# Second layer's front: the half-filled second steps of keys' and values' products side by side in two 64-row tiles, values' product moved behind the keys'

## The reference

```python
# second layer, "front": cross-attention with the context, 16 heads of 16
q = (xn @ Wq + bq);  k = (ctx @ Wk + bk);  v = (ctx @ Wv + bv)     # ctx: [128, 192] per sequence
attn = softmax(q k^T / sqrt(16));  out = attn v
x = x + relu(out @ W1 + b1) @ W2 + b2
# second layer, "cell": six nodes, each attention with 8 heads of 32
for c in range(6):
    q, k, v = (node @ We[edge] + be[edge]) * ew[c]   # three earlier nodes
    node[c] = act_w[c] * mha(q, k, v, Wq[c], Wk[c], Wv[c], Wo[c]) + q
x = x + layernorm(node[5]) * g + b
```

## Time and profile before

| | |
|---|---|
| median of 3 runs | 4046.48 us (4045.95 to 4048.25) |
| profiled execution | 4048.74 us, span 4046.9 us |
| mean granted TensorE clock | 0.995 |
| TensorE busy | 3974.8 us, 98% of the span |
| ScalarE, VectorE, GpSimd busy | 66%, 59%, 46% |

### The profile page before, as it was taken

One profiled execution on the slowest core, in us unless ns is written; L12 is line 12 of the kernel. 1 busy time (PEld: TensorE's weight loads), 2 busy tenths in 40 slices (PEclk: granted clock), 3 DMA queues, 4 the chain that ended last, 5 costly groups with the idle time before them and its releaser, 6 DMA issues.

```text
span 4046.9 us, 100880 instructions
## 1 busy us (share of the span) xinstructions
PE 3974.8 (98%) x38276; PEld 3397.6 (84%) x38276; DVE 2400.2 (59%) x6216; ACT 2651.8 (66%) x11851; POOL 1865.0 (46%) x1979
## 2 busy tenths in 40 slices
PE   8999999999999999999999999999999999999998
PEld 6888876678888888888888888888888888888887
DVE  6888861025566666656666666566666656656654
ACT  8998961125666666666666666666666666666765
POOL 5788872113444444444444444444444444444434
PEclk9999999999999999999999999999999999999999
DMA  3232214520000000000000000000000000000000
GB/s 103 75 105 76 72 52 154 168 78 18 12 14 15 15 14 14 13 17 15 14 13 13 14 13 13 19 13 12 13 12 12 12 12 12 12 12 12 7 4 9
DMA packets 117867, 129.74 MB, mean 32 GB/s; under 512 B 12006, under 2 KB 110676, under 8 KB 117264
## 3 DMA queue, kind: packets, MB, share of 16 engines
q1 hardware_dynamic: 105648, 109.80, 8.5%
q0 software_dynamic: 6144, 8.43, 0.7%
q10 hardware_dynamic: 5600, 5.07, 0.4%
HBM read 89.68 MB, written 41.94 MB: 33 GB/s over the span
## 4 chain that ended last, share of the span: by engine, by line
PE 76%; DVE 1%; ACT 0%; POOL 0%; issue 0%; DMA 0%; POOLq 0%
PE c_product L1552 37%; PE c_product L1563 15%; PE c_product L1611 10%; PE c_scores L1601 7%; PE c_product L1634 5%; PE c_product L1622 2%; DVE c_qT L1407 1%; PE c_product L1540 1%; ACT c_front_probs L1364 0%; PE c_product L1671 0%; DMA out<-c_fin 0%; POOL c_fin L1348 0%; DVE c_nodes L1407 0%; POOL c_front_probs L1318 0%; ACT c_probsT L1370 0%
## 5 line engine op out<-in xcount | busy, mean ns | idle before, releaser
L1318 POOL TENSOR_TENSOR c_probs<-c_probs,c_row_inv 128x512 f32<-128x512 f32 x744 | 770.3, 1045 | 1357.0 <-DVE c_row_inv L1419 1351.4
L1364 ACT ACTIVATE c_probs<-c_scores,c_neg_max 128x128 f32<-128x128 f32 x2976 | 1052.6, 407 | 333.1 <-DVE c_neg_max L1416 332.9
L1552 PE MATMUL c_product<-c_nodes,cell_w 128*128 128x256 f32 x4352 | 1065.2, 383 | 2.8 <-DVE c_nodes L1478 2.4
L1552 PEld LDWEIGHTS c_product<-c_nodes,cell_w 128*128 128x128 f32 x4352 | 796.2, 190 | 121.4 <-DVE c_nodes L1407 8.3
L1416 DVE TENSOR_REDUCE c_neg_max<-c_scores 128x4 f32<-128x512 f32 x1024 | 658.9, 680 | 177.6 <-PE c_scores L1601 170.1
L1364 ACT ACTIVATION_READ_ACCUMULATOR c_probs<-c_scores,c_neg_max 128x1 f32 x2976 | 733.1, 246 | 0.0
L1370 ACT COPY c_probsT<-c_product 128x512 f32<-128x512 f32 x744 | 408.1, 602 | 433.9 <-PE c_product L1611 430.4
L1364 ACT ACTIVATE c_front_probs<-c_scores,c_neg_max 128x128 f32<-128x128 f32 x1120 | 399.6, 398 | 182.5 <-DVE c_neg_max L1416 182.5
L1563 PE MATMUL c_product<-cell_w,c_nodes 128*128 128x256 f32 x1792 | 429.3, 379 | 0.0
L1318 POOL TENSOR_TENSOR c_front_probs<-c_front_probs,c_row_inv 128x512 f32<-128x512 f32 x280 | 295.0, 1057 | 291.0 <-DVE c_row_inv L1419 289.3
L474 ACT ACTIVATE a_probs<-a_scores,a_neg_max 128x128 f32<-128x128 f32 x1024 | 360.4, 409 | 47.4 <-DVE a_neg_max L545 47.0
(11 more groups left out here) (181 smaller groups left out, 6449.7 us busy)
## 6 DMA issues: line engine op xcount, KB each, us to landing
e_w<-in_L_ffn_w SPq DMA_DIRECT2D x12, 1024.0 KB, 6.2
a_x<-in_x SPq DMA_DIRECT2D x32, 256.0 KB, 3.0
a_ctxT<-in_ctx_pairsT SPq DMA_DIRECT2D x32, 256.0 KB, 3.5
x<-a_x SPq DMA_DIRECT2D x32, 256.0 KB, 2.1
xn<-a_xn SPq DMA_DIRECT2D x32, 256.0 KB, 2.2
c_routed<-xn SPq DMA_DIRECT2D x32, 256.0 KB, 2.7
c_x<-x SPq DMA_DIRECT2D x32, 256.0 KB, 3.1
c_ctxT<-in_ctx_pairsT SPq DMA_DIRECT2D x32, 256.0 KB, 2.8
```

The lines of the kernel that those rows point to most:

```text
L1318: nc.gpsimd.tensor_tensor(e, e, rinv[:, i, r].unsqueeze(2).broadcast_to([P, 4, T]), ALU.mult).then_inc(norm_made, 1)
L1364: a = nc.scalar.activation(probs(n, j)[:, r, k], S[r][:, k], ACT.Exp, bias=nmax[:, i, r, k:k + 1], accum_out=rsum[:, i, r, k:k + 1])
L1552: i = T_.matmul(m[:, u], w[:, k, u * P:(u + 1) * P], src[:, k], start=n == 0, stop=n == last)
```

## The change

Three things are changed.

1. **The second steps in pairs.** Where `f.V` of a job stands right behind `f.K`, TensorE first does the two 128-row matmuls of keys' first step (`u` = 0, 1), then the two of values' first step, and then, for u = 0 and 1, one keys' matmul on rows 0 to 63 of the second step and one values' matmul on rows 64 to 127. The two of a pair write different banks. Both products' semaphore counts are raised by their last matmul.
2. **The order.** `f.V` moves from behind `K5` to behind `f.K` on TensorE, and `f.V^` from behind `S4.x3` (in the last turns `K5^`) to behind `f.K^` on VectorE. The heads are made longer so that jobs 0 to 2 keep their order, and job 31 keeps its own in the tail. Jobs 3 to 30 take the paired form. ScalarE's and GpSimd's orders stay.
3. **The layout.** The context's rows 128 to 191 stand twice, in rows 128 to 191 and 192 to 255. `Wk` has its last 64 rows in 128 to 191 and zeros behind them; `Wv` has zeros in 128 to 191 and its last 64 rows in 192 to 255. Sizes stay 256 rows. The first layer reads arrays of the same layout with its old code.

```diff
 PE_ORDER = """
...
-S0:0 O2:1 K3:1 T5.0:2 Q3:1 T5.1:2 V0:0 T0.0:0 S3:1 A5:2 f.K:-1 T0.1:0 O5:2 K1:0 T3.0:1 A0:0 f.Sb0:-1 O0:0 V3:1
-T3.1:1 Q1:0 f.Tb0.0:-1 K4:1 A3:1 S1:0 O3:1 V1:0 Q4:1 T1.0:0 S4:1 T1.1:0 K5:1 f.V:-1 f.Tb0.1:-1 V4:1 A1:0
+S0:0 O2:1 K3:1 T5.0:2 Q3:1 T5.1:2 V0:0 T0.0:0 S3:1 A5:2 f.K:-1 f.V:-1 T0.1:0 O5:2 K1:0 T3.0:1 A0:0 f.Sb0:-1
+O0:0 V3:1 T3.1:1 Q1:0 f.Tb0.0:-1 K4:1 A3:1 S1:0 O3:1 V1:0 Q4:1 T1.0:0 S4:1 T1.1:0 K5:1 f.Tb0.1:-1 V4:1 A1:0
...
 DVE_ORDER = """
...
-S0.i1:1 O2^:2 K3^:2 S5.i3:3 S0.i2:1 S0.i3:1 Q3^:2 S3.x0:2 S3.x1:2 A5^:3 S3.x2:2 S3.i0:2 f.K^:0 S3.i1:2 S3.x3:2
-S3.i2:2 O5^:3 K1^:1 S3.i3:2 A0^:1 f.Sb0.x0:0 f.Sb0.x3:0 f.Sb0.x1:0 f.Sb0.x2:0 f.Sb0.i0:0 O0^:1 f.Sb0.i1:0
...
+S0.i1:1 O2^:2 K3^:2 S5.i3:3 S0.i2:1 S0.i3:1 Q3^:2 S3.x0:2 S3.x1:2 A5^:3 S3.x2:2 S3.i0:2 f.K^:0 f.V^:0 S3.i1:2
+S3.x3:2 S3.i2:2 O5^:3 K1^:1 S3.i3:2 A0^:1 f.Sb0.x0:0 f.Sb0.x3:0 f.Sb0.x1:0 f.Sb0.x2:0 f.Sb0.i0:0 O0^:1
...
                 elif n == "f.K":
                     loaded(pe, c_in, early["ctx0_in"], j)
-                    project(product(n, j), (wk, ct)).then_inc(prod, 1)
+                    if after != ("f.V", j):
+                        project(product(n, j), (wk, ct)).then_inc(prod, 1)
+                    else:
+                        keys_m = product(n, j)
+                        for u in range(2):
+                            T_.matmul(keys_m[:, u], wk[:, 0, u * P:(u + 1) * P], ct[:, 0], start=u == 0, stop=False)
                 elif n == "f.V":
                     loaded(pe, c_in, early["ctx0_in"], j)
-                    project_rows(product(n, j), (wv, ct)).then_inc(prod, 1)
+                    m = product(n, j)
+                    if keys_m is None:
+                        project_rows(m, (wv, ct)).then_inc(prod, 1)
+                    else:
+
+                        for b in range(PAIR):
+                            T_.matmul(m[:, b], ct[:, 0, b * T:(b + 1) * T], wv[:, 0], start=b == 0, stop=False)
+                        for u in range(2):
+                            k = T_.matmul(keys_m[:, u], wk[half[0], 1, u * P:(u + 1) * P], ct[half[0], 1], start=False, stop=u == 1)
+                            v = T_.matmul(m[:, u], ct[half[1], 1, u * T:(u + 1) * T], wv[half[1], 1], start=False, stop=u == 1)
+                        k.then_inc(prod, 1)
+                        v.then_inc(prod, 1)
+                        keys_m = None
...
+    arrays["ctx_pairsT"] = np.ascontiguousarray(np.concatenate([c, c[:, P:]], 1))
...
+        gap = np.zeros_like(wk[P:])
+        arrays[n + "_Wk_rows"] = np.concatenate([wk, gap])
+        arrays[n + "_Wv_rows"] = np.concatenate([wv[:P], gap, wv[P:]])
```

More of the change, by code:

```diff
@@ L966 @@
 f.Txn^:1 S5.i1:3 f.Q^:0 S5.x3:3 Q0^:1 K0^:1 A2^:2 S5.i0:3 S0.x0:1 S0.x3:1 S0.x1:1 S5.i2:3 S0.x2:1 S0.i0:1
-S0.i1:1 O2^:2 K3^:2 S5.i3:3 S0.i2:1 S0.i3:1 Q3^:2 S3.x0:2 S3.x1:2 A5^:3 S3.x2:2 S3.i0:2 f.K^:0 S3.i1:2 S3.x3:2
-S3.i2:2 O5^:3 K1^:1 S3.i3:2 A0^:1 f.Sb0.x0:0 f.Sb0.x3:0 f.Sb0.x1:0 f.Sb0.x2:0 f.Sb0.i0:0 O0^:1 f.Sb0.i1:0
-f.x2:-1 Q1^:1 f.Sb0.i2:0 e.st:3 K4^:2 A3^:2 S1.x2:1 S1.x0:1 S1.i2:1 S1.x1:1 S1.x3:1 O3^:2 S1.i0:1 S1.i1:1
-S1.i3:1 Q4^:2 S4.x0:2 f.Sb0.i3:0 S4.x1:2 S4.x2:2 S4.i0:2 K5^:2 S4.x3:2 f.V^:0 A1^:1 S4.i1:2 f.Sb1.x2:0
+S0.i1:1 O2^:2 K3^:2 S5.i3:3 S0.i2:1 S0.i3:1 Q3^:2 S3.x0:2 S3.x1:2 A5^:3 S3.x2:2 S3.i0:2 f.K^:0 f.V^:0 S3.i1:2
+S3.x3:2 S3.i2:2 O5^:3 K1^:1 S3.i3:2 A0^:1 f.Sb0.x0:0 f.Sb0.x3:0 f.Sb0.x1:0 f.Sb0.x2:0 f.Sb0.i0:0 O0^:1
+f.Sb0.i1:0 f.x2:-1 Q1^:1 f.Sb0.i2:0 e.st:3 K4^:2 A3^:2 S1.x2:1 S1.x0:1 S1.i2:1 S1.x1:1 S1.x3:1 O3^:2 S1.i0:1
+S1.i1:1 S1.i3:1 Q4^:2 S4.x0:2 f.Sb0.i3:0 S4.x1:2 S4.x2:2 S4.i0:2 K5^:2 S4.x3:2 A1^:1 S4.i1:2 f.Sb1.x2:0
 f.Sb1.x3:0 S4.i2:2 f.Sb1.x0:0 f.Sb1.i2:0 f.Sb1.x1:0 f.Ab0^:0 S4.i3:2 f.Sb1.i0:0 O1^:1 f.Sb1.i1:0 K2^:1 e.nm:3
@@ L999 @@
 f.Tb1.1:1 Q2:0 f.Ab1:1 S2:0 f.W1a:1 f.W1b:1 f.Tx:2 f.W2:1 V2:0 B16:0 T2.0:0 f.K:2 f.Txn:1 K0:1 Q0:1 T2.1:0
-S0:1 A2:0 O2:0 B17:0 Q3:0 T0.0:1 S3:0 V3:0 f.Q:2 V0:1 T0.1:1 K1:1 f.Sb0:2 A0:1 T3.0:0 O0:1 T3.1:0
+S0:1 A2:0 O2:0 B17:0 Q3:0 T0.0:1 S3:0 V3:0 f.Q:2 V0:1 T0.1:1 K1:1 f.Sb0:2 A0:1 T3.0:0 O0:1 T3.1:0 Q1:1
+f.Tb0.0:2 K4:0 A3:0 S1:1 O3:0 V1:1 Q4:0 T1.0:1 S4:0 T1.1:1 K5:0 f.V:2
 """
@@ L1068 @@
 f.Q^:2 S5.x3:5 Q0^:3 K0^:3 A2^:4 S0.x0:3 S5.i1:5 S0.x2:3 S5.i0:5 S0.x1:3 S5.i2:5 S0.i2:3 S0.i0:3 O2^:4 S5.i3:5
[L1069 to L1075, removed]
+K3^:4 S0.x3:3 Q3^:4 S0.i1:3 f.x2:1 f.st:1 S3.x0:4 S0.i3:3 S3.x1:4 A5^:5 S3.x3:4 f.K^:2 f.V^:2 S3.i1:4 S3.i0:4
+O5^:5 S3.x2:4 K1^:3 A0^:3 S3.i3:4 f.Sb0.x0:2 S3.i2:4 f.Sb0.x3:2 f.Sb0.x1:2 f.Sb0.x2:2 f.Sb0.i0:2 O0^:3
+f.Sb0.i1:2 Q1^:3 f.Sb0.i2:2 A3^:4 S1.x1:3 S1.x0:3 S1.x2:3 S1.x3:3 S1.i1:3 K4^:4 O3^:4 S1.i0:3 S1.i2:3 e.st:5
+S1.i3:3 Q4^:4 S4.x0:4 S4.x2:4 f.Sb0.i3:2 S4.x3:4 S4.x1:4 S4.i0:4 K5^:4 S4.i2:4 A1^:3 f.Sb1.x0:2 S4.i1:4
+S4.i3:4 f.Sb1.x3:2 f.Ab0^:2 f.Sb1.x1:2 f.Sb1.x2:2 f.Sb1.i3:2 f.Sb1.i0:2 f.Sb1.i1:2 O1^:3 f.Sb1.i2:2 K2^:3
+e.nm:5 Q2^:3 A4^:4 S2.x1:3 S2.x0:3 S2.x2:3 S2.x3:3 O4^:4 f.Ab1^:2 f.x:1 Q5^:4 S2.i0:3 S2.i1:3 f.W1a^:2 f.Tx^:1
+f.W1b^:2 S5.x0:4 S2.i2:3 S5.x3:4 S5.x1:4 f.K^:1 S5.i3:4 f.W2^:2 S5.x2:4 S5.i1:4 S2.i3:3 S5.i0:4 f.Q^:1 f.st3:2
 f.Sb0.x3:1 S5.i2:4 f.Sb0.x1:1 f.Sb0.x0:1 f.nm3:2 f.V^:1 f.Sb0.i3:1 f.Txn^:2 f.Sb0.i0:1 f.Sb0.x2:1 f.Sb0.i1:1
@@ L1576, in node_landed @@
                 landed("f.Txn" if c < 0 else f"O{c}", j)
-            for n, j in on_pe:
+            keys_m = None
+            half = slice(0, P // 2), slice(P // 2, P)
+            for (n, j), after in zip(on_pe, on_pe[1:] + [None]):
                 s = j % JOBS_IN_FLIGHT
@@ L1741 @@
           "L1_ffn_Wo", "L1_ffn_ln_g", "L1_ffn_ln_b"]
-def whole_tiles(a, axis):
-    pad = [(0, -a.shape[i] % P if i == axis else 0) for i in range(a.ndim)]
-    return np.ascontiguousarray(np.pad(a, pad))
 def lay_out(inputs):
@@ L1752, in lay_out @@
     c = arrays.pop("ctx_768")
[L1753 to L1756, removed]
+    c = c.reshape(-1, PAIR, *c.shape[1:]).transpose(0, 3, 1, 2).reshape(c.shape[0] // PAIR, c.shape[2], PAIR * c.shape[1])
+    arrays["ctx_pairsT"] = np.ascontiguousarray(np.concatenate([c, c[:, P:]], 1))
+    for n in ("L0_xattn", "L1_xattn"):
+        wk, wv = arrays.pop(n + "_Wk"), arrays.pop(n + "_Wv")
+        gap = np.zeros_like(wk[P:])
+        arrays[n + "_Wk_rows"] = np.concatenate([wk, gap])
+        arrays[n + "_Wv_rows"] = np.concatenate([wv[:P], gap, wv[P:]])
     arrays["mask_BxS2_bf1"] = np.ascontiguousarray(inputs["mask_BxS2_bf1"]).view(np.uint8)
```

## The result

The changed kernel takes 4101.07 us (median of four runs, 4099.79 to 4101.29) against 4046.22 us (4044.94 to 4048.25) for the kernel before in the same measurement: a ratio of 1.0134, 95% interval 1.0117 to 1.0152. The profiled execution took 4101.22 us, its span is 4099.4 us, and the mean granted clock is 0.994 (0.995 before). The forecast was 4097 us. One run stands apart from all others: the fourth run of experiment 7 took 6789.92 us at a mean granted clock of 0.554, and that experiment's ratio and times leave it out.

The account below looks back on a forecast made before the run. TensorE's chain of steps was taken to bound the kernel. Per job, -0.51 + 1.22 + 1.08 = +1.79 us, times 28 is +50.1 us, from 4046.5 to 4096.6 us; range 4060 to 4111, the forecast's own 4085 to 4108.

Parts of the forecast that it names:

- The saving of the pairs: On TensorE at `f.K` and `f.V`, pairing 64-row matmuls saves 0.51 us per job net of tiling changes.
- full overlap: The two 64-row tiles of a pair run side by side on TensorE, saving four records' time, 0.86 us per job.
- the changes of tiling: Entering 64-row tiling once more and returning from it costs TensorE 0.34 us per job.
- The wait at `O5`: TensorE's `O5` waits 1.12 us for VectorE's `f.K^` to free its bank; 1.22 us per job with the weight load.
- the hand-over: Time from the end of `f.K^` on VectorE until the waiting `O5` goes on, taken as 0.05 us.
- The unhidden weight load: After its wait, `O5`'s first weight load is not hidden on TensorE: 0.10 us per job.
- The wait at `f.Sb1`: With `f.V` gone from ahead of it, `f.Sb1` on TensorE waits for ScalarE's exponentials of `S4`: 1.08 us per job.
- The next context's load: SyncE's load leaves about 34 us earlier, has the whole job to land, and changes nothing.
- Only one of the waits: Rival: only the wait at `O5` (+0.71 us per job, 4066 us) or at `f.Sb1` (+0.57, 4063 us) comes; chance 0.12.
- Neither wait lasts: Rival: banks are freed before TensorE asks, so the saving stays: 14 us faster, 4032 us; chance 0.05.
- The tiles don't overlap: Rival: the pairs on TensorE run one after another, 2.22 us more per job, 4109 us; chance 0.07.

Follow-up runs that it names:

- experiment 7: The changed kernel with, in 26 of 28 jobs, both `O5` ahead of `T0.1` and `K2` at `f.V`'s old place: 4068.79 us, ratio 1.0051 (three runs).
- experiment 2: The changed kernel with the pairs' order kept but every matmul of them over all 128 rows, so no tiling: 4108.84 us, ratio 1.0155.
- experiment 3: The changed kernel with both matmuls of a pair on rows 0 to 63, so they can't run side by side: 4112.57 us, ratio 1.0158.
- experiment 4: The changed kernel with `O5` ahead of `T0.1` in 26 of 28 jobs, and three steps of `S3` moved on other engines: 4068.70 us, ratio 1.0056.
- experiment 5: The changed kernel with `O5` ahead of `T0.1` as in experiment 4, but both products in full unpaired form: 4077.45 us, ratio 1.0076.
- experiment 8: The changed kernel with VectorE doing `f.V^` ahead of `f.K^`: 4128.89 us, ratio 1.0203.
- experiment 1: The changed kernel with its new order and layout, but both products in full 128-row form, not interleaved: 4079.00 us, ratio 1.0080.
- experiment 6: The changed kernel with `K2` put at `f.V`'s old place, ahead of `f.Tb0.1`, in 26 of 28 jobs: 4102.65 us, ratio 1.0133.
- experiment 9: The kernel before the change with only the new layout of the context, `Wk` and `Wv`: 4046.72 us, ratio 1.0001.

## Why the prediction was right, step by step

| per job, us | predicted | measured | from |
|---|---|---|---|
| `f.K` to `T0.1` | 3.56 to 2.99: -0.57 | 2989.45 - 2986.46 = 2.99: -0.57 | after |
| `T0.1` to `O5` (0.87 before) | 2.05: +1.18 | 2991.60 - 2989.45 = 2.15: +1.28 | after |
| `O5` to `K1` (3.46 before) | +0.10 | 2995.13 - 2991.60 = 3.53: +0.07 | after |
| `f.Sb1` to `f.Ab0` (1.10 before) | +1.08 | 2.25: +1.15 | after |
| sum | +1.79 | +1.93 (99.50 - 97.58 = 1.92) | |

- **The saving of the pairs.** Right in each part: full overlap (0.85 of 0.86 us) and the changes of tiling (0.28 us up to `T0.1`'s start), by experiments 2 and 3. The prediction took these prices from the rounds of scores and the column tiles, and they held for the 64-row tiles. The net 0.51 becomes 0.47 where a projection follows the pairs and not transposes (0.10 in place of 0.06), and experiments 4 and 5 measure 0.45.
- **The wait at `O5`.** Right in place, releaser and size. The term that was too small is the hand-over. `f.K^` ends at 2990.92 + 0.53 = 2991.45 and `O5` starts at 2991.60, so 0.15 us lie between and not 0.05. In experiment 8, behind a longer wait, it is 0.15 us again (3007.63 + 0.54 = 3008.17 to 3008.32). The 0.05 was read from `S4` at 2982.83, a round of scores, and `O5` is a projection; `f.Sb1`, a round of scores too, goes on after 0.05 us also behind a real wait (3029.35 to 3029.40). Which of the two a step takes was not known from the rows of before. The chain's row of 0.14 us at 2991.46 is this time. The unhidden weight load was a little too large a term: `O5` itself is 0.07 longer and not 0.10.
- **The wait at `f.Sb1`.** Right, by experiment 1 for its size alone (1.15 us with nothing else changed) and by experiment 6, where the filler takes it away. It was 0.07 too small for another reason than at `O5`. The prediction let ScalarE's chain end with the last exponential, at 2991.33. The matmuls wait for the accumulator read behind it, which before the change ends at 2991.43 (the row of 2991.11 shown above). With this end the same working gives 1.18 us, and 1.15 was measured. The hand-over of 0.05 us was right here.
- **The rest.** The next context's load leaves at 2989.59, 3.1 us behind `f.K`'s start; the prediction had it leave some 34 us earlier and cost nothing. `K1` doesn't wait for `f.V^`, and `f.Ab0` doesn't wait behind `f.Tb0`'s copies. Layout and loads cost nothing (experiment 9). The busy share fell to 98.3%, and the clock stayed.
- **The rivals.** "Only one of the waits" is what experiment 4 builds: 98.275 - 97.58 = 0.69 us a job where this rival had 0.57, and 4068.7 us where it had 4063 over two jobs more. "Neither wait lasts" is what experiment 7 was to build, and the second wait came back elsewhere. "The tiles don't overlap" is experiment 3.

The sizes missed are +0.10 (hand-over), -0.03 (weight load) and +0.07 (accumulator read). By the jobs' period they make 0.13 us a job, 3.6 of the 4.5 us between the 4096.6 of the sum and the measurement, so the number owes next to nothing to errors that cancel.

One thing the prediction didn't say in so many words is why the pairing is the cause of the first wait: with the order alone it isn't there (experiment 1). The pairing saves 0.45 us a job where nothing waits for its results (experiments 4 and 5). In this order it costs 99.50 - 98.73 = 0.77, since the keys' last matmul comes right ahead of `T0.1` and `O5` waits until VectorE's four instructions of `f.K^` are through. The two of `f.V^` stand behind them and cost nothing; put first, they cost 0.71 us more (experiment 8).

What stays open is whether any order keeps the pairs' 0.45 us with neither wait. Only one filler was tried, and it had no slack at its own place.
